# A graph network's five layers: normalisation joined with the next layer's inputs, first edge tiles loaded earlier, no block that clears semaphores

## The reference, cut to what matters

```python
deg = zeros(n).at[row].add(1.0) + 1.0
dinv = deg ** (-0.5)
norm = (dinv[row] * dinv[col])[:, None]
h = input_feature
for l in range(5):
    xl = h @ W[l] + b[l]
    ee = edge_attr @ We[l] + be[l]
    msg = norm * relu(xl[row] + ee)
    agg = zeros_like(xl).at[col].add(msg)
    conv = agg + relu(xl + root[l]) / deg[:, None]
    mean, var = conv.mean(axis=0), conv.var(axis=0)
    hbn = (conv - mean) * rsqrt(var + 1e-5) * gamma[l] + beta[l]
    if l < 4:
        hbn = relu(hbn)
    h = hbn + h
```

## Time and profile before

| | us |
|---|---|
| median of 3 runs | 6801.9 |
| the profiled execution, its own time | 6786.33 |
| its span, from the first to the last instruction | 6784.7 |
| of it, the five edge stages | 3573.0 |
| of it, one passage from the last edge tile of a layer to the first gather of the next | 65.1 to 66.0, four times |

### The profile page before, as it was taken

How to read it: one execution, slowest core, us unless ns; L and a number is a source line. 1 busy time by engine, 2 the same in 40 slices (tenths; PEclk the granted TensorE clock), 3 DMA queues, 4 the chain that set the end, 5 groups by cost and what they waited for, 6 DMA issues and landing times. The chain is left out here.

```text
span 6784.7 us, 97259 instructions
## 1 busy us (share of the span) xinstructions
PE 4343.0 (64%) x21805; PEld 3583.0 (53%) x21806; DVE 3048.1 (45%) x6902; ACT 1972.4 (29%) x4303; POOL 2764.5 (41%) x3021
## 2 busy tenths in 40 slices
PE   4666643652996467775776566675676757775392
PEld 3444433542885356664666555564565646664261
DVE  4433457752001645554454544455454445555303
ACT  1111110010231034442444434442444424444120
POOL 2444422533002155553555445553555535553101
PEclk8787766975998588887888788887888878887596
DMA  4555563632453144442444344343443424442131
GB/s 137 158 160 156 159 190 95 176 91 79 184 192 127 35 125 122 116 121 87 116 123 116 88 121 114 108 118 92 116 115 109 117 87 119 121 116 72 47 108 53
DMA packets 461211, 794.76 MB, mean 117 GB/s; under 512 B 221403, under 2 KB 278412, under 8 KB 450551
## 3 DMA queue, kind: packets, MB, share of 16 engines
q0 software_dynamic: 130720, 364.17, 19.4%
q1 hardware_dynamic: 322967, 401.22, 19.0%
q10 hardware_dynamic: 7488, 28.97, 1.4%
HBM read 671.50 MB, written 123.52 MB: 117 GB/s over the span
## 5 line engine op out<-in xcount | busy, mean ns | idle before, releaser
L1730 POOL DMA_INDIRECT g_g<-xl_table,g_idx x2080 | 1968.0, 946 | 1663.3 <-issue 1146.3
L1774 PE MATMUL g_b<-g_onehot,g_msg 128*128 128x128 f32 x8320 | 1375.9, 319 | 893.3 <-DVE agg L1862 336.4
L1774 PEld LDWEIGHTS g_b<-g_onehot,g_msg 128*128 128x128 f32 x8320 | 1296.6, 229 | 1109.8 <-DVE agg L1862 796.8
L1862 DVE TENSOR_TENSOR agg<-agg,g_b 128x256 f32 x2080 | 868.0, 417 | 1331.8 <-remote 854.0
L1761 PE MATMUL g_b<-g_we,g_ea 128*128 128x256 f32 x4160 | 1291.4, 441 | 185.9 <-DVE g_msg L1849 92.4
L1761 PEld LDWEIGHTS g_b<-g_we,g_ea 128*128 128x128 f32 x4160 | 844.8, 225 | 302.0 <-DVE g_msg L1849 112.9
L1833 ACT ACTIVATE g_msg<-g_msg 128x512 f32<-128x512 f32 x1040 | 650.8, 626 | 1124.5 <-DVE g_msg L1849 1002.7
L1849 DVE TENSOR_TENSOR g_msg<-g_g,g_b 128x512 f32<-128x512 f32 x1040 | 710.4, 683 | 483.4 <-remote 222.2
L544 PE MATMUL sc_pe_h<-ae_h_rows,sc_onehot 128*128 x1664 | 506.9, 456 | 218.5 <-DVE sc_prod L616 152.4
L512 POOL DMA_INDIRECT sc_g<-h_table,sc_idx x416 | 399.5, 960 | 452.9 <-DVE sc_alpha L608 330.0
L544 PEld LDWEIGHTS sc_pe_h<-ae_h_rows,sc_onehot 128*128 128x128 f32 x1664 | 348.4, 220 | 332.1 <-issue 272.7
(11 more groups left out here) (256 smaller groups left out, 3536.0 us busy)
## 6 DMA issues: line engine op xcount, KB each, us to landing
g_ea<-in_ea SPq DMA_DIRECT2D x260, 512.0 KB
ex_w<-in_f_w SPq DMA_DIRECT2D x80, 1024.0 KB, 7.4
e_rows<-sc_g SPq DMA_DIRECT2D x208, 272.0 KB
g_g<-xl_table,g_idx POOLq DMA_INDIRECT x2080
at_g<-e_rows ACTq DMA_DIRECT2D x52, 544.0 KB, 4.0
at_g<-e_rows SPq DMA_DIRECT2D x52, 544.0 KB, 3.7
xl_table<-g_rows SPq DMA_DIRECT2D x25, 640.0 KB, 4.0
sc_rel<-rel_row SPq DMA_DIRECT2D x52, 256.0 KB
```

The costliest lines, as they stand in the source:

```text
L1730: nc.gpsimd.indirect_dma_start(out=g.g[:, j, :], out_offset=None, in_=k.xl_table[:, :], in_offset=bass.IndirectOffsetOnAxis(ap=g.idx[:, q, ...
L1774: last = nc.tensor.matmul(ps[u % (SB // 2)][:, at:at + P], g.msg[:, j, b * P:(b + 1) * P], g.onehot[:, j, :], start=True, stop=True)
L1862: nc.vector.tensor_tensor(window, window, ps[u % (SB // 2)][:, i * D:(i + 1) * D] .rearrange("p (b n) -> p b n", b=K), ALU.add).then_inc(g ...
```

## The change

1. `graph_next_inputs` takes the place of `graph_layer_norm` and the next `graph_layer_inputs`: one block instead of two. ACT and DVE go through the pieces in column order (both feature blocks of columns 0 to 511, then of 512 to 1023, and so on), and PE starts the node tiles of a piece when both blocks of it are updated. DVE's bias adds of a piece stand behind the update of the piece that follows. The weights are loaded at the head of this block. The next layer's `cols` would overwrite gamma and beta, so these are loaded again into a tile of their own.
2. POOL sets `k.agg` to zero only when all 14 updates are done.
3. The first two halves of indices and edge features are loaded in the block of the inputs, behind the weights, and no longer at the top of the edges.
4. The clearing block is gone. POOL clears 12 semaphores at the head of `graph_next_inputs`, SP clears 13 at the head of the edges. Those of the index and feature loads count on over the layers, so POOL's and PE's waits for them contain `l * (16 * ITERS)` now.
5. The first layer's inputs and edges stand before the loop, the last norm behind it; the edge code is there twice.

```diff
+def load_first_half_tiles(k, sp):
+    a, g = k.a, k.gl
+    for q in range(2):
+        sp.dma_start(g.idx[:, q, :], a["src_halves"][q]).then_inc(g.idx_in[q], 16)
+        sp.dma_start(g.ea[:, q, :], a["ea128"][:, q * HALF * P:(q + 1) * HALF * P]).then_inc(g.ea_in[q], 16)
...
 def graph_layer_inputs(k, l):
...
         sp.dma_start(g.we[:], a["g1_we"][bass.ds(l * P, P), :]).then_inc(g.weights, 16)
+        load_first_half_tiles(k, sp)
         for s in range(NSTEP):
...
-def graph_layer_edges(k, l):
+def graph_layer_edges(k, l, tag):
...
-        for q in range(2):
-            load_rows(q, places(q, 0)[0])
-            load_features(q, places(q, 0)[1])
+        for s in g.of_nodes:
+            sp.sem_clear(s)
...
-                pool.wait_ge(g.idx_in[u // (HALF // 2)], 16)
+                pool.wait_ge(g.idx_in[u // (HALF // 2)], l * (16 * ITERS) + 16)
...
-                    pool.wait_ge(g.idx_in[u // (HALF // 2)], it * 16 + 16)
+                    pool.wait_ge(g.idx_in[u // (HALF // 2)], it * 16 + l * (16 * ITERS) + 16)
...
-                pe.wait_ge(g.ea_in[u // (HALF // 2)], it * 16 + 16)
+                pe.wait_ge(g.ea_in[u // (HALF // 2)], it * 16 + l * (16 * ITERS) + 16)
...
+def graph_next_inputs(k, l):
...
+    @block.sync
+    def _(sp):
+        nxt = bass.ds(l * P + P, P)
+        sp.dma_start(g.cols_before[:], a["g1_cols"][bass.ds(l * P, P), :]).then_inc(g.weights, 16)
+        sp.dma_start(w[:], a["g1_w"][nxt, :].rearrange("p (b d) -> p b d", b=K)).then_inc(g.weights, 16)
...
+        sp.dma_start(g.we[:], a["g1_we"][nxt, :]).then_inc(g.weights, 16)
+        load_first_half_tiles(k, sp)
+        for i in range(NSTEP):
+            sp.wait_ge(g.biased, STEP * (i + 1))
+            sp.dma_start(tile_rows(k.xl_table, i * STEP, STEP, 0, D), row[:, i % 2, :, :]).then_inc(g.stored[i % 2], 16)
...
+    @block.vector
+    def _(dve):
...
+        dve.wait_ge(g.stat, K * len(parts) + K)
+        dve.wait_ge(g.weights, 80)
+        v.tensor_tensor(g.rowb[:], g.bias[:, 0:D], g.bias[:, D:2 * D], ALU.add).then_inc(g.summed_bias, 1)
+        v.tensor_tensor(g.rootb[:], g.cols[:, 0:K], g.cols[:, K:2 * K], ALU.add).then_inc(g.summed_bias, 1)
+        dve.wait_ge(g.root, 1)
...
+        def bias_tile(t):
+            i = t // STEP
+            if t % STEP == 0 and i >= 2:
+                dve.wait_ge(g.stored[i % 2], 16 * (i // 2))
+            dve.wait_ge(g.xl_ready, t + 1)
+            v.tensor_tensor(row[:, i % 2, t % STEP, :], tb[t % 4][:, 0:D], g.rowb[:], ALU.add).then_inc(g.biased, 1)
+
+        t = 0
+        for n, (at, width) in enumerate(CHUNKS):
+            for b in range(K):
+                dve.wait_ge(g.scaled, n * K + b + 1)
+                v.scalar_tensor_tensor(out=k.h[:, b, at:at + width], in0=k.agg[:, b, at:at + width],
+                                       scalar=k.floor[:, bass.ds(l, 1)], in1=k.h[:, b, at:at + width],
+                                       op0=ALU.max, op1=ALU.add).then_inc(g.updated, 1)
+            while n >= 1 and t < n * TILES:
+                bias_tile(t)
+                t += 1
+        while t < NT:
+            bias_tile(t)
+            t += 1
...
+    @block.tensor
+    def _(pe):
+        pe.wait_ge(g.weights, 80)
+        for t in range(NT):
+            pe.wait_ge(g.updated, K * (t // TILES) + K)
+            if t >= 4:
+                pe.wait_ge(g.biased, t - 3)
...
+    @block.gpsimd
+    def _(pool):
+        for e in g.of_edges:
+            pool.sem_clear(e)
+        pool.wait_ge(g.updated, K * len(CHUNKS))
+        nc.gpsimd.memset(k.agg[:], 0.0).then_inc(g.cleared_agg, 1)
...
 def graph_layers(k):
...
-        with nc.Fori(0, LAYERS) as l:
-            graph_layer_inputs(k, l)
-            graph_layer_edges(k, l)
-            graph_layer_norm(k, l)
-            with nc.Block() as block:
-                @block.gpsimd
-                def _(pool):
-                    for s in g.cleared:
-                        pool.sem_clear(s)
+        k.gl = GraphLayers(k, c)
+        graph_layer_inputs(k, 0)
+        graph_layer_edges(k, 0, "first")
+        with nc.Fori(0, LAYERS - 1) as l:
+            graph_next_inputs(k, l)
+            graph_layer_edges(k, l + 1, "next")
+        graph_layer_norm(k, LAYERS - 1)
```

More of the change, by code:

```diff
@@ L1836, in _ @@
     def _(dve):
-        base_regs = [dve.alloc_register(f"g1_base{i}") for i in range(BODY)]
+        base_regs = [dve.alloc_register(f"g1_{tag}_base{i}") for i in range(BODY)]
         dve.sem_inc(g.raw, EB)
@@ L1958, in graph_layer_norm, with _ @@
     g.close()
+def graph_next_inputs(k, l):
+    nc, a, g = k.nc, k.a, k.gl
+    stats, mv, s = g.stats, g.mv, g.scale
+    parts = [(i, min(CHUNK, N - i)) for i in range(0, N, CHUNK)]
+    w, row, tb = g.w, g.rows, g.banks[0:4]
+    TILES = CHUNK // P
+    block = g.open()
+    @block.sync
[3 more added lines that the diff above has]
+        sp.dma_start(w[:], a["g1_w"][nxt, :].rearrange("p (b d) -> p b d", b=K)).then_inc(g.weights, 16)
+        sp.dma_start(g.bias[:], a["g1_bias"][bass.ds(l + 1, 1), :].broadcast_to([P, 2 * D])).then_inc(g.weights, 16)
+        sp.dma_start(g.cols[:], a["g1_cols"][nxt, :]).then_inc(g.weights, 16)
+        sp.dma_start(g.we[:], a["g1_we"][nxt, :]).then_inc(g.weights, 16)
[3 more added lines that the diff above has]
+            sp.dma_start(tile_rows(k.xl_table, i * STEP, STEP, 0, D), row[:, i % 2, :, :]).then_inc(g.stored[i % 2], 16)
+        for i in range(2):
+            sp.wait_ge(g.stored[i], 16 * ((NSTEP + 1 - i) // 2))
+    @block.vector
+    def _(dve):
+        v = nc.vector
+        for b in range(K):
+            for n, (at, width) in enumerate(CHUNKS):
+                v.tensor_tensor(k.agg[:, b, at:at + width], k.agg[:, b, at:at + width], k.dinv_row[:, at:at + width],
+                                ALU.mult).then_inc(g.conv, 1)
+        for b in range(K):
+            for n, (at, width) in enumerate(parts):
+                dve.wait_ge(g.conv, b * len(CHUNKS) + n + 1)
+                v.bn_stats(stats[:, b, n, :], k.agg[:, b, at:at + width]).then_inc(g.stat, 1)
+        for b in range(K):
+            dve.wait_ge(g.stat, (b + 1) * len(parts))
+            v.bn_aggr(mv[:, b, :], stats[:, b, :, :].rearrange("p n s -> p (n s)")).then_inc(g.stat, 1)
+            dve.wait_ge(g.stat, (b + 1) * len(parts))
+        dve.wait_ge(g.stat, K * len(parts) + K)
[3 more added lines that the diff above has]
+        dve.wait_ge(g.root, 1)
+        v.reciprocal(s[:, 0, :], s[:, 0, :]).then_inc(g.step, 1)
+        dve.wait_ge(g.step, 1)
+        v.tensor_tensor(s[:, 0, :], s[:, 0, :], g.cols_before[:, 2 * K:3 * K], ALU.mult).then_inc(g.step, 1)
+        dve.wait_ge(g.step, 2)
+        v.tensor_tensor(s[:, 1, :], s[:, 0, :], mv[:, :, 0], ALU.mult).then_inc(g.step, 1)
+        dve.wait_ge(g.step, 3)
+        v.tensor_tensor(s[:, 1, :], g.cols_before[:, 3 * K:4 * K], s[:, 1, :], ALU.subtract).then_inc(g.step, 1)
+        dve.wait_ge(g.summed_bias, 2)
+        def bias_tile(t):
[5 more added lines that the diff above has]
+        t = 0
+        for n, (at, width) in enumerate(CHUNKS):
+            for b in range(K):
+                dve.wait_ge(g.scaled, n * K + b + 1)
[8 more added lines that the diff above has]
+            t += 1
+        dve.wait_ge(g.updated, K * len(CHUNKS))
+    @block.scalar
+    def _(act):
+        act.wait_ge(g.stat, K * len(parts) + K)
+        nc.scalar.activation(s[:, 0, :], mv[:, :, 1], ACT.Sqrt, bias=k.eps[:, 0:1]).then_inc(g.root, 1)
+        act.wait_ge(g.step, 4)
+        for at, width in CHUNKS:
+            for b in range(K):
+                nc.scalar.activation(k.agg[:, b, at:at + width], k.agg[:, b, at:at + width], ACT.Identity,
+                                     bias=s[:, 1, b:b + 1], scale=s[:, 0, b:b + 1]).then_inc(g.scaled, 1)
+    @block.tensor
[5 more added lines that the diff above has]
+                pe.wait_ge(g.biased, t - 3)
+            for kk in range(K):
+                last = nc.tensor.matmul(tb[t % 4][:, 0:D], k.h[:, kk, t * P:(t + 1) * P], w[:, kk, :],
+                                        start=(kk == 0), stop=(kk == K - 1))
+            last.then_inc(g.xl_ready, 1)
+    @block.gpsimd
[4 more added lines that the diff above has]
+        nc.gpsimd.memset(k.agg[:], 0.0).then_inc(g.cleared_agg, 1)
+        pool.wait_ge(g.cleared_agg, 1)
+    g.close()
@@ L1982, in __init__ @@
         self.ea_in = [sem(f"ea_in{i}") for i in range(2)]
[L1983 to L1989, removed]
+        (self.weights, self.xl_ready, self.biased, self.summed_bias, self.cleared_agg, self.conv, self.stat, self.root,
+         self.step, self.scaled, self.updated) = nodes = [sem(n) for n in (
+             "weights", "xl_ready", "biased", "summed_bias", "cleared_agg", "conv", "stat", "root",
+             "step", "scaled", "updated")]
+        (self.xlt_ready, self.rooted, self.started, self.begun, self.raw, self.product, self.hot, self.relu, self.summed,
```

(4 more changed lines are left out.)

2 lines of the change are left out of this document (1 added, 1 removed).

## The result

The changed kernel takes 6743.69 us (median of four, 6729.37 to 6753.3) against 6811.45 (median of four, 6800.92 to 6824.63): a ratio of 0.9898, with a 95% interval from 0.9869 to 0.9926, so about 68 us less; the interval allows 50 to 89. The forecast was 6732, 69.6 less, with a range from 6708 to 6764.

A forecast was written before the change was run, and what follows sets the result against it. At each passage one engine bounds each part, with no overlap and waits for clearing, weights and indices; 4 x (15.2 + 1.65) plus 1.65 plus 2.1 less 1.6 gives 69.6 us off 6801.9: 6732, range 6708 to 6764.

The forecast's parts named there:

- PE's start: Passage between layers: tile 0 starts after two updates instead of fourteen, at 3114.0 instead of 3129.19, 15.2 us earlier.
- The feed: Node tiles: PE stays fed between pieces and runs its 25 tiles in 24.60 us as before; cost put at nothing.
- Rival 1: Node tiles: PE starves between pieces and stays at 1.2 GHz, 65 us in all, 6797, no change; chance 0.03.
- Rival 4: Passages: PE starts only after all updates, losing 7.6 of the 15.2 us in each, 6762; chance 0.05.
- The memset: POOL's memset after the last update: 5.64 us, ends about 2.8 us ahead of the next block, so hidden.
- First tiles: Start of the edges: early index and feature loads remove the wait before the first gather, 1.65 us per layer.
- Clearing and loop: Layer boundaries: no clearing block gains 2.1 us behind the last norm; three loop steps and the exit cost 1.6 us.
- Longer waits: Edge iterations: one more register instruction in POOL's and PE's two waits; put at nothing, bounds 0 and +6.7 us.
- Rival 3: Edge loop's second copy runs worse: change loses from 0.54 us an iteration, 6868 if iterations grow 1.05; chance 0.02.
- Rival 2: Edge stages shift: 67 us less (6665) or 69 more (6801, no change); chance 0.06 down, 0.04 up.

The follow-up runs named there:

- the two undoing runs: Changed kernel with PE waiting for all updates: 5526.49 us, ratio 0.9928; then weights also loaded only after the last update: passages 60.55 to 62.23 us.
- The one run aimed at the stops: Changed kernel with each edge-feature load in the edge loop bringing only 16 of 1024 columns: 5504.05 us, edge stages 531.0 to 531.7 us.

## Why the prediction was right

The mechanism was right, and the passages show it: 16.55 us less in each on average, where 15.2 + 1.65 = 16.85 were forecast. That the totals agree to 2 us is in part luck, since their interval allows 50 to 89 us. The absolute 6732 is 12 below the measured 6743.69, and 9.6 of that lie in the median it started from, 6801.9 of three runs where four give 6811.45.

*PE's start.* 15.2 us was the largest term, and 15.1, 14.8, 15.0 and 14.8 were measured on the first chip. Its working was right in each step, as the two undoing runs show: 7.45 for the order, 4.6 for the weights, and 3.0 that remain for the clearing, its barriers and the step back. The bias sums cost 0.1 as said.

*The feed.* I put it at nothing, and it costs nothing that shows: at the high clock PE is busy for 21.85 of 21.90 us with the updates beside it. On the first chip PE's start to the last bias add is 23.9 us on average, before and after. Rival 1, a PE that stays at 1.2 GHz, didn't come: 0.93 in the window of the node tiles, with the first tiles slow as before. Rival 4 would have shown as PE's start at +27.

*The memset.* Hidden, as forecast, but by 2.0 us and not by 2.8. The step that failed is where I let the cover end: at the next block's first instruction instead of at the barrier ahead of it.

*First tiles.* 1.65 us was forecast for each layer. 1.65 was measured in the first, 1.6 in the other four from the last bias add to the first gather (7.3 us before, 5.7 after), and taking it back gave 1.5. That DVE's first message add comes up to 0.5 us sooner behind the gather was missed, to the good.

*Clearing and loop.* Behind the last norm 2.1 us were forecast and 2.1 measured (ACT's idle time, 3.77 and 1.69). The loop's step back was charged with 0.4 us, three times and once more for the exit, 1.6 in all. DVE's idle time before the first multiply shows what it is: 0.53 to 0.54 before; after, 0.68 where the loop is entered (the earlier trace rows and its counterpart above), 0.97 or 0.98 behind each of the three steps back, and 0.68 behind the exit:

```profile
3893.84 1.29 DVE L2001 TENSOR_TENSOR agg<-agg,dinv_row 128x512 f32<-128x512 f32 x2 [0.98 <-PEq L2119]
```

```profile
6196.40 0.69 DVE L1927 TENSOR_TENSOR agg<-agg,dinv_row 128x512 f32<-128x512 f32 x1 [0.68 <-PEq L2119]
```

So a step back costs 0.44 us, and entry and exit 0.15 each: 1.6 us in all, as charged.

*Longer waits.* Put at nothing with 6.7 as bound. Without the loop's 1.6 the edge stages are 2.2 us longer on the quicker chip, no more than variants with the same edge code differ by.

*Rival 3.* Its threshold was mis-worked, with no effect on the result: I divided by 130 iterations, but the second copy of the edge loop and the longer waits stand in four of the five layers, 104 iterations. The loss would have begun at 0.67 us an iteration, not at 0.54, and the known part is 0.06.

*Rival 2.* It was the right thing to widen the range for. On the slower chip the edge stages took 15 us more after than before, and without that the profiled execution would have stood 48 instead of 33 us lower. But the layers there vary without any change in the code, and on the quicker chip they hardly vary (529.7 to 531.4). So the 15 us are no effect of the change, as far as these runs can tell, but for the loop's 1.6.

## What to carry to other kernels

At a boundary between stages, write down for each engine when its first instruction could run by its data, and compare that with the trace: here PE needed a sixth of the columns, the loads needed nothing, and 15 of 34 us were in that difference. Such a gain is a number of microseconds, so read it in windows around the boundary, where it shows to half a microsecond, and not in the total of one execution. Before handing half of an elementwise step to POOL, look whether DVE's part has two SBUF inputs too; before a burst of matmuls behind a long idle time, a few extra ones on idle PE bring the clock up, if they end in time.

## What the runs showed of the hardware that I had not expected

- The same kernel takes 6811 to 6816 us on some chips and 5566 to 5573 on others. Nearly all of the extra time lies in the edge stages, 700 to 732 us instead of 530 each, and ahead of the graph layers, 2358 instead of 2069; behind the last edge stage it is 556.6 against 553.5. The granted clock in an edge stage is 0.84 there and 0.97 here. The one run aimed at the stops landed on a chip without them, but the trace of before tells their order. In its five edge stages PE stops 118 times for over 3 us, 576 us in all, and in all but six of these it had the high clock in its last microsecond of work; on the quicker chip, in the kernel before, it never stops so long in an edge stage. The first stop of the second edge stage (two windows, columns as told above) begins at the high level, and the clock falls behind it:

```profile
3174.00:3178.50 4.50, 0.00 (x0) 0.00 (x0) 0.00 (x0) 0.00 (x0) 3.28 (x5) 0.97 0.35 95
3178.70:3181.10 2.40, 0.00 (x0) 0.00 (x0) 0.68 (x1) 0.00 (x0) 1.79 (x3) 0.50 0.37 103
```

So the low clock doesn't begin the stops, though it adds time behind them (four of the feature matmuls take 2.08 us behind this stop and 1.03 ahead of it). What does begin them stays open.
- On the quicker chips the edge loop seems to be bound by POOL's issue of indirect DMAs, 0.95 us each and 0.30 between them: 520 of 531 us. That is read from the waits; no run changed the issue.
- Clearing a semaphore takes 0.04 us on POOL; but 29 of them in a block of their own, with its barriers and the loop's step back, put off PE's start by 3.0 us.
